# Layer 0's heads: stacked projection in two products, and a query behind the exponentials

## What is computed

```python
q_c = hidden_size @ Wq_c.T + bq_c
q = (q_c @ Wq_up.T + bq_up).reshape(b, s, NH, Q_HEAD).transpose(0, 2, 1, 3)
kv = hidden_size @ Wkv_c.T + bkv_c
kv_nope, kv_rope = (kv[..., :KV_LORA], kv[..., KV_LORA:])
kvu = (kv_nope @ Wkv_up.T + bkv_up).reshape(b, s, NH, QK_NOPE + V_HEAD).transpose(0, 2, 1, 3)
k_nope, v = (kvu[..., :QK_NOPE], kvu[..., QK_NOPE:])
...
scores = jnp.einsum('bhqd,bhkd->bhqk', q, k) / np.sqrt(Q_HEAD)
attn = jax.nn.softmax(scores, axis=-1)
o = jnp.einsum('bhqk,bhkv->bhqv', attn, v)
out = jnp.einsum('bhsv,Hv->bsH', o, Wo) + bo
```

## Time and profile before

| | before |
|---|---|
| median of 3 runs | 1567.95 us (1567.38 to 1568.76) |
| profiled execution, span | 1564.7 us |
| PE busy | 1503.2 us, 96% |
| DVE busy | 1098.6 us, 70% |
| ACT busy | 771.0 us, 49% |
| POOL busy | 475.6 us, 30% |

### The profile page before, as it was taken

How to read it: one execution, slowest core, us unless ns; L and a number is a source line. 1 busy time by engine, 2 the same in 40 slices (tenths; PEclk the granted TensorE clock), 3 DMA queues, 4 the chain that set the end, 5 groups by cost and what they waited for, 6 DMA issues and landing times. The chain is left out here.

```text
span 1564.7 us, 29168 instructions
## 1 busy us (share of the span) xinstructions
PE 1503.2 (96%) x9057; PEld 1320.1 (84%) x9057; DVE 1098.6 (70%) x2790; ACT 771.0 (49%) x2153; POOL 475.6 (30%) x505
## 2 busy tenths in 40 slices
PE   6999999999689989999999999999999999999898
PEld 5899999998367777888889888888888888988776
DVE  3788888888486756666676666666666667666765
ACT  3777878787345534434444444344443444444521
POOL 3445454545231013113213213312311321321321
PEclk9999999999799999999999999999999999999999
DMA  4111111111144440111011011011011101100001
GB/s 162 37 57 46 55 48 53 52 49 46 55 140 145 133 148 8 48 54 39 15 54 54 0 54 54 0 54 54 12 41 54 44 9 54 54 0 13 1 14 41
DMA packets 42833, 80.20 MB, mean 51 GB/s; under 512 B 5040, under 2 KB 13744, under 8 KB 42800
## 3 DMA queue, kind: packets, MB, share of 16 engines
q1 hardware_dynamic: 42800, 79.77, 16.8%
HBM read 77.66 MB, written 2.10 MB: 51 GB/s over the span
## 5 line engine op out<-in xcount | busy, mean ns | idle before, releaser
L98 PE MATMUL c_bj<-g_xT_hi,b_w 128*128 128x512 f32 x512 | 214.6, 419 | 2.8 <-PEq L901 2.8
L99 PE MATMUL c_bj<-g_xT_lo,b_w 128*128 128x512 f32 x512 | 203.3, 397 | 0.0
L100 PE MATMUL c_bj<-g_xT_hi,b_w 128*128 128x512 f32 x512 | 203.0, 397 | 0.0
L438 POOL TENSOR_TENSOR h_pr<-h_pr,h_rinv 128x512 f32<-128x512 f32 x128 | 133.2, 1041 | 159.9 <-DVE h_rinv L529 157.5
L1119 POOL CAST b_w<-b_raw_q 128x512 fp32r<-128x512 f32 x32 | 20.5, 640 | 435.8 <-PE c_bj L100 435.8
L98 PE MATMUL c_bj<-b_w,g_xT_hi 128*128 128x256 f32 x512 | 143.2, 280 | 0.0
L99 PE MATMUL c_bj<-b_w,g_xT_hi 128*128 128x256 f32 x512 | 143.2, 280 | 0.0
L100 PE MATMUL c_bj<-b_w,g_xT_lo 128*128 128x256 f32 x512 | 142.7, 279 | 0.0
L468 ACT ACTIVATE h_pr<-h_bs,h_nmax 128x256 f32<-128x256 f32 x256 | 118.8, 474 | 3.0 <-DVE h_nmax L524 2.1
L1351 DVE TENSOR_TENSOR c_v_lo<-c_bj,c_v_hi 128x256 fp32r<-128x256 f32 x128 | 54.3, 424 | 93.9 <-ACT c_v_hi L1263 93.9
L1247 ACT ACTIVATE c_o<-c_bo 128x128 f32<-128x128 f32 x128 | 35.5, 277 | 171.2 <-PE c_bo L1465 171.2
(11 more groups left out here) (266 smaller groups left out, 4663.8 us busy)
## 6 DMA issues: line engine op xcount, KB each, us to landing
f_wi<-in_w_ffn SPq DMA_DIRECT2D x66, 256.0 KB, 2.6
h_part<-in_w_ffn SPq DMA_DIRECT2D x32, 264.0 KB, 2.8
b_raw_q<-in_w_attn SPq DMA_DIRECT2D x32, 256.0 KB, 6.8
b_raw_k<-in_w_attn SPq DMA_DIRECT2D x32, 256.0 KB, 7.3
b_raw_v<-in_w_attn SPq DMA_DIRECT2D x16, 512.0 KB, 7.6
b_raw_o<-in_w_attn SPq DMA_DIRECT2D x16, 512.0 KB, 3.9
a_w<-in_w_head SPq DMA_DIRECT2D x32, 225.0 KB, 2.8
e_wraw<-in_w_ffn SPq DMA_DIRECT2D x1, 2304.0 KB, 8.4
```

Source lines behind the costliest of these rows:

```text
L98: pe.matmul(out, w[0], x[0], start=start, stop=False, skip_group_check=True)
L99: pe.matmul(out, w[0], x[1], start=False, stop=False, skip_group_check=True)
L100: return pe.matmul(out, w[1], x[0], start=False, stop=stop, skip_group_check=True)
L438: pool.tensor_tensor(pr[b][:, :, :], pr[b][:, :, :], rinv[b][:, :][:, :, None].to_broadcast([P, 2, S]), ALU.mult)\
```

## The change

Five things are changed, all in `attention0_heads`:
- The projection takes two products. The first is rounded weights by rounded values, as before. The second is stacked: its weights `wv_mix` hold the rounded part in partitions 0 to 63 and the rest in 64 to 127, and its values `o_mix` hold the rest in 0 to 63 and a copy of the rounded part of 0 to 63 in 64 to 127. What this drops against three products: the rest of partitions 64 to 127 by the rounded weights, and their rounded part by the rest of the weights.
- SP makes that copy with a DMA inside SBUF (`duplicate`, 128 KB), two a head; the projection waits for it (`s_odup`). VectorE's `outs` works on partitions 0 to 63 alone.
- Both projections of a head come two heads later (rounds 0 and 2 of head h do head h - 2); before, that of round 2 did head h - 1. Two rounds are added at the end. GpSimd splits the value weights in round 3 in place of 1, with one more copy, and SP's order is written anew.
- ScalarE's query of round 2 stands behind the probabilities and exponentials of that round in place of ahead of them.
- VectorE's query of round 2 moves to round 3, behind that round's maxes; the reduction of the integer block moves from round 3 to round 2.

```diff
@@ run
-            round_(NH + 1, 0)
+            for b in range(3):
+                round_(NH + 1, b)
@@ sync
+                def duplicate(p, par):
+                    sp.wait_ge(s_ohi, p + 1)
+                    sp.dma_start(f32(o[par][1][KVL:P, :]), f32(o[par][0][0:KVL, :])).then_inc(s_odup[par], 16)
+
+                def ahead(h):
+                    if has(h - 3, NH):
+                        duplicate(2 * h - 6, 0)
+                    if has(h, NH):
+                        fetch(h)
+                    if has(h - 2, NH):
+                        fetch_wv(h - 2)
+                    if has(h - 3, NH):
+                        duplicate(2 * h - 5, 1)
+                    if has(h - 1, NH):
+                        fetch_part(h - 1)
@@ gpsimd, split_wv
-                    pool.tensor_tensor(wvs[1][:, :], wv[:, :], f32(wvs[0][:, :]), ALU.subtract).then_inc(s_wvl, 1)
+                    plain(pool, s_tick)
+                    pool.tensor_copy(wvs[1][0:KVL, :], wv[0:KVL, :]).then_inc(s_wvl, 1)
+                    pool.wait_ge(s_wvl, 2 * h + 1)
+                    pool.tensor_tensor(wvs[1][KVL:P, :], wv[KVL:P, :], f32(wvs[0][KVL:P, :]), ALU.subtract)\
+                        .then_inc(s_wvl, 1)
+                    pool.wait_ge(s_wvl, 2 * h + 2)
@@ gpsimd, round_
-                    if b == 1 and has(h - 1, NH):
+                    if b == 3 and has(h - 1, NH):
                         split_wv(h - 1)
@@ scalar, round_
-                    if b == 2 and has(2 * h + 2, NPAIR):
-                        query(2 * h + 2, 0)
...
                     if has(s, NS):
                         exps(s, b)
+                    if b == 2 and has(2 * h + 2, NPAIR):
+                        query(2 * h + 2, 0)
@@ vector, outs
-                    dve.tensor_tensor(o[par][1][:, :], bo[:, :], f32(o[par][0][:, :]), ALU.subtract)\
+                    dve.tensor_tensor(o[par][1][0:KVL, :], bo[0:KVL, :], f32(o[par][0][0:KVL, :]), ALU.subtract)\
@@ vector, round_
-                    if b == 2 and has(2 * h + 2, NPAIR):
+                    if b == 3 and has(2 * h + 2, NPAIR):
                         query(2 * h + 2, 0)
...
-                    if b == 3 and has(h, NH):
+                    if b == 2 and has(h, NH):
                         dve.wait_ge(s_part, 16 * h + 16)
@@ tensor
                 def project(h, p, c):
                     pe.wait_ge(s_olo, p + 1)
-                    pe.wait_ge(s_wvl, h + 1)
-                    matmul3(pe, acc[c][:, :], (wvs[0][:, :], wvs[1][:, :]), (o[c][0][:, :], o[c][1][:, :]), False,
-                            False).then_inc(s_om, 1)
+                    pe.wait_ge(s_odup[c], 16 * (h + 1))
+                    pe.wait_ge(s_wvl, 2 * h + 2)
+                    pe.matmul(acc[c][:, :], wvs[0][:, :], o[c][0][:, :], start=False, stop=False,
+                              skip_group_check=True)
+                    pe.matmul(acc[c][:, :], wvs[1][:, :], o[c][1][:, :], start=False, stop=False,
+                              skip_group_check=True).then_inc(s_om, 1)
@@ tensor, round_
-                    if b == 0 and has(h - 2, NH):
-                        project(h - 2, 2 * h - 3, 1)
-                    if b == 2 and has(h - 1, NH):
-                        project(h - 1, 2 * h - 2, 0)
+                    if b % 2 == 0 and has(h - 2, NH):
+                        project(h - 2, 2 * h - 4 + b // 2, b // 2)
```

More of the change, by code:

```diff
@@ L350, in attention0_heads @@
         s_part, s_mag = k.sem("part_in"), k.sem("mag")
-        wvs = (t.sb("wv_hi", [P, VH], F32R), t.sb("wv_lo", [P, VH], F32R))
+        wvs = (t.sb("wv_hi", [P, VH], F32R), t.sb("wv_mix", [P, VH], F32R))
         gm = t.sb("gm", [P, 2, P])
@@ L355, in attention0_heads @@
         q = [(t.sb(f"q{i}_hi", [P, HALF], F32R), t.sb(f"q{i}_lo", [P, HALF], F32R)) for i in range(2)]
-        o = [(t.sb(f"o{i}_hi", [P, HALF], F32R), t.sb(f"o{i}_lo", [P, HALF], F32R)) for i in range(2)]
+        o = [(t.sb(f"o{i}_hi", [P, HALF], F32R), t.sb(f"o{i}_mix", [P, HALF], F32R)) for i in range(2)]
         pr = [t.sb(f"pr{i}", [P, 2, S]) for i in range(NB)]
@@ L372, in attention0_heads @@
         s_pv, s_ohi, s_olo = k.sem("pv"), k.sem("o_hi"), k.sem("o_lo")
-        s_wvh, s_wvl, s_om = k.sem("wv_hi"), k.sem("wv_lo"), k.sem("om")
+        s_wvh, s_wvl, s_om = k.sem("wv_hi"), k.sem("wv_mix"), k.sem("om")
+        s_odup = [k.sem(f"o_dup{i}") for i in range(2)]
         def run(eng, round_):
@@ L397, in fetch_wv @@
                 def fetch_wv(h):
-                    need(sp, s_wvl, h)
+                    need(sp, s_wvl, 2 * h)
                     sp.dma_start(wv[:, :], io["wv_head0"][bass.ds(h, 1), :, :].rearrange("a p n -> (a p) n"))\
@@ L405, in fetch_part @@
                       .then_inc(s_part, 16)
[L407 to L414, removed]
+                def duplicate(p, par):
[12 more added lines that the diff above has]
+                        fetch_part(h - 1)
+                fetch(1)
+                fetch_part(0)
+                ahead(2)
+                with sp.Fori(3, NH) as h:
+                    ahead(h)
+                for h in range(NH, NH + 3):
+                    ahead(h)
             @block.gpsimd
```

## The result

The changed kernel takes 1580.33 us (median, 1579.28 to 1581.91) against 1567.66 us (1565.68 to 1568.76) for the kernel before: ratio 1.0079, with a 95% interval of 1.0064 to 1.0093. The change makes the kernel slower by 12.7 us. The profiled execution has a span of 1577.7 us. The forecast was 1576.4 us with a range of 1569.5 to 1581.5, so the result lies inside it, near the upper edge.

What follows compares the result with a forecast made beforehand. TensorE was taken to bound layer 0's heads, with 0.14 us a head lost waiting for exponentials. Up to the last head +8.9, tail -0.5: +8.4 us on span 1564.7, 1573.1; plus 3.25 gives 1576.4 us, range 1569.5 to 1581.5.

Steps and rivals of the forecast that it cites:

- The step that decided: Round 3, TensorE's next-head scores: they wait 0.8 us for VectorE's moved query rest, starting 0.52 us later than before.
- The chain from merge to `q_lo`: VectorE, from the merge at 208.34 through reciprocals, maxes and probabilities to the query rest's end at 214.66.
- the release: Round 3, TensorE: the weight load starts 0.11 us after VectorE ends the query's rest.
- The products: TensorE, rounds 0 and 2: one product of 0.23 us fewer in each; only round 0's saving is kept.
- the 15 that I gave as a sign: Profile after the change: TensorE's busy time should fall by about 15 us.
- Exponentials: ScalarE, round 2: they start 0.03 us after the maxes, take 1.02 us and end 1.00 us earlier than before.
- The moved reduction: VectorE, round 2: the integer block's maximum, 0.61 us to the reciprocal, lies in a wait and costs about 0.02.
- Last heads: End of the heads' stage: -0.47 - 0.6 - 0.86 + 1.4 = -0.5 us, bounds -1.2 and +1.0.
- GpSimd's split moves to round 3: nothing.: GpSimd, round 3: the weights' split ends near 215.8, is used near 217.6, and costs nothing.
- My first rival: Round 3: TensorE would not wait for the query's rest, saving 0.61 us a head, about 1548 us; chance 0.10.
- The 3.25 us: Whole kernel: the median of the runs lies 3.25 us above the profiled span, added to 1573.1 to give 1576.4.
- my rival on the clock: Heads' stage: TensorE's idle time lowers its clock, costing 0.9 us a head, 27 in all, 1603 us; chance 0.02.

Runs made afterwards that it cites:

- the order alone: Kernel before with three products, only ScalarE's query behind the exponentials and VectorE's query in round 3, block reduction left in round 3: ratio 1.0114, period 11.68 us.
- the old order: Changed kernel with two products, but query, exponentials and block reduction back in their old places on ScalarE and VectorE: ratio 0.9991, period 11.02 us.
- query behind the probabilities: Changed kernel with ScalarE's round 2 as probabilities, query, exponentials and VectorE's as maxes, probabilities, query, block: ratio 0.9964, period 10.88 us.

## Why the prediction was right, and where it was not

**The mechanism.** The step that decided was that the scores of round 3 wait for the query's rest, which stands behind the reciprocal and the maxima. The rows of after show that wait 23 times in the stretch, and the order alone brings it while the old order removes it. The chain from merge to `q_lo` was worked out as 6.32 us and is 6.36; the release as 0.11 and is 0.12. The links of VectorE's queue are 0.61, 0.60, 0.60 and 0.60, where the prediction had put 0.59, 0.60, 0.61 and 0.58; its own rows have 0.58 and 0.59 for the first two, a slip of 0.01 each that lay on the right side. So the period is 11.45 and not 11.40. This term was mis-sized by 0.05 us a head, 1.5 us over 30 heads. Merge of head 0 to merge of head 31 grew by 10.1 us where +8.9 was forecast.

**The products.** 0.23 us a head for round 0 and nothing for round 2: both shown, by the pair 11.68 and 11.45 and by the wait, 0.44 and 0.67. TensorE's busy time fell by 8.1 us and not by the 15 that I gave as a sign. Part of the wait is still counted as busy: the record of the last product ahead of it reaches over its start, so that TensorE shows 0.67 us idle where its weight loads show 0.88. In one head the modelled busy time is 10.78 of 11.45 us, against 11.11 of 11.11 before.

**Exponentials.** They start 0.04 us after the end of the maxima (216.20 + 0.69 = 216.89, then 216.93) and end 1.02 us later, as placed. The wait of the earlier trace rows for them is gone, in favour of the longer one.

**The moved reduction** on VectorE costs nearly nothing: reciprocal at 218.01, which the exponentials' end at 217.95 would have allowed at 217.98. That holds only because SP asks for the block earlier; without it the reduction costs 0.60 us a head.

**Last heads.** Forecast -0.5, measured -0.7 as the mean of two profiles. That they agree is partly luck. From the merge of head 31 to the values' products that wait for the last but one copy (the first and third of the rows below) I had put -1.07 (a product in each of two rounds, and the reduction), and the first profiles show 22.45 and 22.26 us, -0.2. From there to the output stage I had put +0.5, and they show 6.38 and 5.64 us, -0.7: before, this stretch ran at the half clock from 398 us on, and in the changed kernel it ran at the full one up to 412 us.

```profile
397.39 0.36 PE L622 MATMUL h_bo<-h_pt_hi,a_cs 128*128 128x256 f32 x1 [1.50 <-DVE h_o_lo L538]
```

```profile
398.00:403.00 5.00, 3.59 (x12) 2.62 (x10) 0.69 (x1) 0.60 (x1) 0.00 (x0) 0.50 0.00 0
```

```profile
407.09 0.36 PE L646 MATMUL h_bo<-h_pt_hi,a_cs 128*128 128x256 f32 x1 [1.50 <-DVE h_o_mix L562]
```

```profile
398.00:412.00 14.00, 8.70 (x52) 6.55 (x52) 7.11 (x14) 6.15 (x18) 5.12 (x9) 1.00 0.18 43
```

The first two of these rows are of the kernel before, the other two of the changed one; the rows by stretch have the columns of the earlier trace rows. The end of the chain in the changed kernel, TensorE's last two projections and ScalarE's last copy:

```profile
409.86 0.47 PE L655 MATMUL a_acc<-h_o_hi,h_wv_hi 128*128 128x512 f32 x1 [1.11 <-POOL h_wv_mix L456]
...
411.69 0.47 PE L655 MATMUL a_acc<-h_o_hi,h_wv_hi 128*128 128x512 f32 x1 [1.13 <-issue]
```

```profile
408.79 0.60 ACT L503 ACTIVATE h_o_hi<-h_bo 128x512 fp32r<-128x512 f32 x1 [2.07 <-PE h_bo L646]
```

From copy to product it is 2.90 us, forecast 2.8; the duplicate takes 2.2 us from issue to landing, not 2.0:

```profile
h_o_mix<-h_o_hi SPq DMA_DIRECT2D x64, 128.0 KB, 2.2
```

The page "DMA: Bandwidth & Descriptors" of the Trainium skill ("Anatomy of one DMA") has a fixed part and the bytes on top, 2.3 us as an estimate. The section is about DMAs that GpSimd issues, while SP issues these. For this transfer it was nearer than my choice of 2.0, and the 64 KB from HBM at 1.7 us still lie below its fixed part. The wait for the split at 409.86 was not in my working; it lies beside the duplicate's transfer, whose product starts only at 411.69, so it is not on the chain that ends last.

**What I got wrong without paying for it.** "GpSimd's split moves to round 3: nothing." I had placed its end and its use by TensorE, but not the normalising that now stands behind it on GpSimd. The wait for `q_lo` covered it in the changed kernel; once that wait is gone it costs 0.12 us a head (old order) to 0.35 (query behind the probabilities). My first rival's saving of 0.61 us a head could therefore not have landed by mending VectorE's order alone: that run gave 0.23, and 0.58 only with the split changed too.

**The rest of the span.** I had put nothing there. The mean spans differ by 12.8 us and the forecast was 8.4; of the 4.4 us between them 2.7 are in this rest, 0.7 ahead of the heads, 1.2 in the heads and -0.2 behind the last merge. They go with the longer time at the half clock there; part of it differs between executions of one kernel, as the second profile of before showed. The code there is the same, but that does not make the time the same, and this term should have had a bound of its own. The 3.25 us that I added to get from span to median compared two executions: the profiled execution of the changed kernel itself took 1579.45 us as timed, only 1.75 above its span.

**The clock.** TensorE's weight loads stood idle for 0.88 us in every 11.45, and the granted clock of the stretch stayed at 1.00, the 2.4 GHz level. The rule of the page "TensorE: Matmul & The Clock Gate" of the Trainium skill ("A second HAM failure mode: psum-queue depth-cycling"), that frequent short idle times let the clock swing, did not show in the heads of this kernel. One argument of my rival on the clock was half a reading, though. I took the stretch of before from 390 to 398 us, busy 4.76 of 8.00 us at 0.99, as proof that a less busy stretch keeps the full level. The clock fell right behind it: it is 0.50 from 398 to 403 us. In the heads of the changed kernel TensorE shows 10.78 us busy of every 11.45 at 1.00; how much more idle time the clock would have borne was not tried.

## What to carry to other kernels

Where engines run in-order queues, follow the loop from one fixed event to itself and add start-to-start times along it; an operation moved behind a waiting one joins that loop, and the idle share of its engine says nothing about it. Work saved ahead of the place where the loop is joined is lost; only work saved behind it counts. When a step moves on any engine, look at what stands behind it there, and then at what that feeds: a cost hidden now is the next bound when the first wait is gone. And before a difference of some us is laid to an edit, compare the time at each clock level in the stretches that the edit did not touch.

## What was not expected of the hardware

- Behind a wait of GpSimd for its own last instruction the idle time differs. In the split it was 0.08 us between the copy and the subtraction (213.64 + 0.29 = 213.93, then 214.01), but 0.45 between the subtraction on 64 partitions and the normalising behind it, whose reciprocal was long done (211.38 + 0.46 = 211.84, then 212.29). In the form of the split without that wait the normalising starts even before the recorded end of the split (208.23 + 0.46 = 208.69, then 208.64). That the wait alone makes the difference, and why this one costs so much more, wasn't tested.
- Half the partitions were no cheaper on GpSimd here: the subtraction takes 0.46 us on 64 partitions by 128 columns, and 0.46 on 128 by 128.
- Two executions of the same program differ by 2.8 us in a part of 1160 us in which nothing was changed, and twelve profiles with the same code there range over 4.5 us, in the order of their time at the half clock but for differences of some tenths. With one profile of each kernel, a difference of this size behind the edited stage can't be laid to the edit.
